# Second mixture of experts: three quarters of its routing moved into the attention stage before it, and its gathers cut into groups of eight

## The reference, cut to what matters

```python
# fifth: causal attention, 16 heads of 16, keys and values from the first 512 rows of ctx
q, k, v = layernorm(x) @ Wq.T + bq, ctx @ Wk.T + bk, ctx @ Wv.T + bv
x = x + softmax(mask(q @ k.T / 4)) @ v @ Wo.T + bo
# sixth: mixture of 8 experts, every row goes to its two best, and a shared expert for all rows
xf = layernorm(x).reshape(2048, 256)
shared = gelu(xf @ Wfc_s + bfc_s) @ Wproj_s + bproj_s            # hidden width 1024
topk_p, topk_i = top_k(softmax(xf @ Wr), 2); gate = topk_p / sum(topk_p)
routed = sum over e of gate[:, e] * (gelu(xf @ Wfc[e] + bfc[e]) @ Wproj[e] + bproj[e])
x = x + shared + routed
```

## Time and profile before

| | us |
|---|---|
| median of 3 runs | 3063.31 (3052.5 to 3068.39) |
| the profiled execution | 3049.62 |
| its span, first to last instruction | 3047.9 |
| attention stage's last addition to `x` ends | 2540.8 |
| first matmul on a shared item | 2564.8 |
| last (fifth) early shared item done | 2673.5 |
| first and last routed tile copied out | 2709.3, 2978.2 |
| last shared item done | 3033.1 |

### The profile page before, as it was taken

How to read it: one execution, slowest core, us unless ns; L and a number is a source line. 1 busy time by engine, 2 the same in 40 slices (tenths; PEclk the granted TensorE clock), 3 DMA queues, 4 the chain that set the end, 5 groups by cost and what they waited for, 6 DMA issues and landing times.

```text
span 3047.9 us, 31366 instructions
## 1 busy us (share of the span) xinstructions
PE 2437.6 (80%) x10876; PEld 1587.8 (52%) x10876; DVE 2186.9 (72%) x3129; ACT 1445.5 (47%) x2547; POOL 888.9 (29%) x614
## 2 busy tenths in 40 slices
PE   4988886478888899938982798897669797699996
PEld 1333432367766566727872234333224345689995
DVE  5999999598886564337885799999845443467775
ACT  5656563145554222214653665665214344256672
POOL 2778776000000000020002487777402121400004
PEclk8999999799999899968995899999968877789997
DMA  4033030700000000022421220312075400236652
GB/s 163 2 110 110 1 112 0 243 22 1 22 1 1 33 1 1 0 102 104 140 80 56 111 97 14 111 43 69 28 153 111 89 2 30 104 129 220 222 204 87
DMA packets 89233, 238.55 MB, mean 78 GB/s; under 512 B 9474, under 2 KB 52879, under 8 KB 81256
## 3 DMA queue, kind: packets, MB, share of 16 engines
q1 hardware_dynamic: 72708, 211.64, 21.6%
q0 software_dynamic: 4608, 12.59, 1.3%
q10 hardware_dynamic: 11760, 12.32, 1.3%
HBM read 194.42 MB, written 42.09 MB: 78 GB/s over the span
## 4 chain that ended last, share of the span: by engine, by line
PE 46%; DVE 28%; ACT 10%; issue 9%; DMA 3%; POOL 3%; ACTq 1%; SPq 1%; DVEq 0%; POOLq 0%
DVE psum L633 10%; PE psum L107 6%; PE psum L108 6%; PE psum L109 6%; PE psum L430 5%; PE psum L114 3%; DVE ch L641 3%; PE psum L395 2%; PE psum L1233 2%; PE psum L1247 2%; ACT g L3024 2%; PE psum L1217 2%; PE psum L1195 1%; PE psum L2358 1%; ACT WH L2874 1%
## 5 line engine op out<-in xcount | busy, mean ns | idle before, releaser
L315 POOL TENSOR_TENSOR bu<-u,row 128x1024 f32<-128x1024 f32 x254 | 597.8, 2358 | 288.0 <-DVE psum L633 189.1
L430 PE MATMUL psum<-ch,ident 128*128 128x512 f32 x1024 | 511.3, 628 | 138.8 <-DVE ch L641 138.2
L633 DVE TENSOR_TENSOR_SCAN psum<-psum,bu 128x1024 f32<-128x1024 f32 x256 | 585.4, 2287 | 19.0 <-ACT psum L512 18.8
L430 PEld LDWEIGHTS psum<-ch,ident 128*128 128x128 f32 x1024 | 188.6, 196 | 428.2 <-DVE ch L641 246.0
L512 ACT ACTIVATE psum<-dt,A 128x511 f32<-128x511 f32 x512 | 332.3, 682 | 0.4
L641 DVE TENSOR_TENSOR ch<-psum,row 128x1024 f32<-128x1024 f32 x256 | 313.0, 1223 | 7.6
L1503 POOL IOTA i<- 128x128 f32 x2 | 0.7, 346 | 766.6 <-DVEq L3172 766.6
L3024 ACT ACTIVATE g<-psum,bias 128x256 f32<-128x256 f32 x248 | 101.2, 471 | 210.3 <-PE psum L109 130.5
L395 PE MATMUL psum<-hT,inw 128*128 128x512 f32 x256 | 138.2, 672 | 43.2 <-ACT sz L472 27.3
L107 PE MATMUL psum<-WH,hs 128*128 128x256 f32 x496 | 145.2, 293 | 15.0 <-DVE hs L3109 6.0
L3109 DVE TENSOR_TENSOR hs<-g,hs 128x512 fp32r<-128x512 f32 x124 | 85.9, 693 | 91.1 <-ACT hs L3031 82.6
(11 more groups left out here) (376 smaller groups left out, 5885.8 us busy)
## 6 DMA issues: line engine op xcount, KB each, us to landing
W<-in_m1W SPq DMA_DIRECT2D x25, 2052.0 KB, 8.7
row<-Ascr SPq DMA_DIRECT2D x64, 512.0 KB, 4.8
row<-Bscr SPq DMA_DIRECT2D x64, 512.0 KB, 4.8
W<-in_m0W SPq DMA_DIRECT2D x16, 1024.0 KB, 9.3
k<-x1scr SPq DMA_DIRECT2D x16, 384.0 KB, 6.7
q<-x1scr SPq DMA_DIRECT2D x16, 384.0 KB, 9.2
x1scr<-hi SPq DMA_DIRECT2D x48, 128.0 KB, 2.4
m1buf<-zt SPq DMA_DIRECT2D x23, 256.0 KB, 3.5
```

The costliest lines, as they stand in the source:

```text
L315: e.tensor_tensor(m.bu[i % 3][:, :, :], u, m.row[:, g, 0, :, :], ALU.mult).then_inc(*m.fed.up)
L430: p = pe.matmul(m.y, k.ident, m.ch[i % RING_C][:, j, :], start=False, stop=g == UNITS - 1 and j == 1)
L633: dve.tensor_tensor_scan(flat, flat, m.bu[i % 3][:, :, :].rearrange("p a n -> p (a n)"), 0.0, ALU.mult, ALU.add).then_inc(*m.scan.up)
```

## The change

- The DRAM buffer `m1buf` has room for all 2048 rows for each expert (`ROOM`), and 256 more. The slot of a row is then `2048 * expert + rank`, and needs only the batches up to its own. Clearing it, early in the kernel, takes 16,640 rows instead of 5,888.
- For batches 0, 1 and 2 the layer norm, the logits, the two best, the ranks and the scatter stand inside the attention stage: units "r" (turn), "l" (logits), "n" (ranks) of batch b-1 in period b, and eight scatters on POOL in the slots of `X1_SENT`. The order of the other units in period 1 is new (`x1_period`): the maxima are woven in faster at the end, keys and queries come later. In period 3 the units spread over 22 slots instead of 14.
- The shared expert's weights are loaded and split in period 3 (`X1_SPLITS`). `WH` shares its space with one set of queries and keys.
- The mixture stage begins with the norm of the last batch only; its routing is for that batch, with eight scatters. `EARLY` is 3 instead of 5, so that five shared items stand behind the routed ones. The turn of the first routed tile moved behind the bias of the gates. SP reads the place of each tile's rows from `rsi`.
- All gathers have buffers of their own. They go out in four groups of eight; three of the groups wait for a place in the shared items. The additions on DVE are four tiles behind each of the last four shared items, instead of three behind each of the last three and seven at the end.

```diff
+ROOM = N
...
+    for j in range(E + 1):
+        n = min(ROOM, ROOM * E + 256 - ROOM * j) // 128
+        sp.dma_start(k.DR["m1buf"][ROOM * j:ROOM * j + 128 * n, :].rearrange("(t p) c -> p t c", p=128),
+                     k.zt[:, 0:1, :].to_broadcast([128, n, D])).then_inc(*k.cleared["m1"].up)
...
+def route_rows_dve(k, m, dve, b):
+    dve.wait_ge(*k.inv_dev(20 + b))
+    for t in range(4 * b, 4 * b + 4):
+        normed(dve, m.FN[:, t, :], k.X[:, t, :], k.xmv, k.xrs, t).then_inc(*m.fn_in.up)
+def logits_pe(k, m, pe, rT, bank):
+    for t in range(4):
+        for j in range(2):
+            p = pe.matmul(bank[:, E * t:E * t + E], rT[:, j, 128 * t:128 * t + 128], m.wr[:, j, :], start=j == 0, stop=j == 1)
+    return p
...
+def marks_dve(k, m, dve, b):
+    v = k.v
+    s = slice(4 * b, 4 * b + 4)
+    o1, o2 = m.oo[:, 0, s, :], m.oo[:, 1, s, :]
+    first_of_four_dve(k, m, dve, m.lg[:, s, :], m.m1[:, s], o1)
+    dve.scalar_tensor_tensor(out=m.l2[:, :, :], in0=o1, scalar=-3e38, in1=m.lg[:, s, :], op0=ALU.mult, op1=ALU.add).then_inc(*v.up)
...
+    first_of_four_dve(k, m, dve, m.l2[:, :, :], m.m2[:, :], o2)
+    dve.tensor_tensor(m.both[:, s, :], o1, o2, ALU.add).then_inc(*m.marks.up)
+    dve.tensor_tensor(m.lg[:, s, :], m.lg[:, s, :], wide4(m.m1[:, s]), ALU.subtract).then_inc(*m.below.up)
+def ranks1_pe(k, m, pe, b, bank):
+    pe.wait_ge(*m.marks(b))
+    rows = m.both[:, 4 * b:4 * b + 4, :].rearrange("p t e -> p (t e)")
+    pe.matmul(bank[:, 0:32], m.tri[:, :], rows, start=True, stop=True)
+    return pe.matmul(bank[:, 32:64], m.ones[:, :], rows, start=True, stop=True)
+def slots_dve(k, m, dve, b, bank, signal):
+    v = k.v
+    for t in range(4):
+        n = 4 * b + t
+        dve.tensor_tensor(m.tot[:, n + 1, :], m.tot[:, n, :], bank[:, 32 + E * t:32 + E * t + E], ALU.add).then_inc(*v.up)
+        dve.wait_ge(*v.last())
+    s = slice(4 * b, 4 * b + 4)
+    dve.tensor_tensor(m.rk[:, :, :], m.tot[:, s, :], bank[:, 0:32].rearrange("p (t e) -> p t e", e=E), ALU.add).then_inc(*signal.up)
+    dve.wait_ge(*signal.last())
+    dve.tensor_tensor(m.two[:, :, :, :], m.oo[:, :, s, :], m.rk[:, :, :].unsqueeze(1).to_broadcast([128, 2, 4, E]), ALU.mult).then_inc(*v.up)
+    dve.wait_ge(*v.last())
+    dve.tensor_reduce(m.sl[:, :, s], m.two[:, :, :, :], AX, ALU.add).then_inc(*v.up)
+    dve.wait_ge(*v.last())
+    dve.tensor_copy(m.si[:, :, s], m.sl[:, :, s]).then_inc(*m.put.up)
+def scatter_pool(k, m, pool, b, i):
+    t, j = 4 * b + i // 2, i % 2
+    if i == 0:
+        if b == 0:
+            pool.wait_ge(*k.cleared["m1"](E))
+        pool.wait_ge(*m.fn_in(4 * b + 3))
+        pool.wait_ge(*m.put(b))
+    pool.indirect_dma_start(k.DR["m1buf"], bass.IndirectOffsetOnAxis(ap=m.si[:, j, t:t + 1], axis=0), m.FN[:, t, :], None) \
+        .then_inc(*m.sent.up)
...
+PAUSE = ("-", 0, 0)
+def x1_routing(b):
+    return [("r", b, 0), ("r", b, 1)], [("l", b, 0)], [("n", b, 0)]
 def x1_period(b):
-    end = x1_end(b - 1) if b else x1_values(1)
-    ahead = x1_keys(b + 2) + x1_queries(b + 2) + x1_values(b + 2) if b + 2 < B else []
-    return x1_woven(x1_maxima(b + 1) if b + 1 < B else [], end + ahead)
+    maxima = x1_maxima(b + 1) if b + 1 < B else []
+    if b == 0:
+        return x1_woven(maxima, x1_values(1) + x1_keys(2) + x1_queries(2) + x1_values(2))
+    turned, logits, ranks = x1_routing(b - 1)
+    if b + 2 < B:
+        q, kk = x1_queries(b + 2), x1_keys(b + 2)
+        rest = turned + kk[0:1] + logits + kk[1:2] + q[0:2] + ranks + q[2:4] + x1_values(b + 2)
+        return x1_woven(maxima[0:24], x1_end(b - 1)) + x1_woven(maxima[24:], rest, 4)
+    return x1_woven(maxima, x1_end(b - 1) + 2 * [PAUSE] + turned + [PAUSE] + logits + 3 * [PAUSE] + ranks)
...
-X1_LAST = [28, 28, 28, 14]
+X1_LAST = [28, 28, 28, 22]
...
+X1_SPLITS = [20, 22, 24, 26]
+X1_SENT = {(b + 1, 28 + i): (b, i) for b in range(2) for i in range(4)}
+X1_SENT.update({(b + 2, i): (b, 4 + i) for b in range(2) for i in range(4)})
+X1_SENT.update({(B - 1, 24 + i): (B - 2, i) for i in range(8)})
...
+    elif w == "r":
+        for t in range(4):
+            pe.wait_ge(*k.route.fn_in(4 * b + t))
+            p = turn_in(k, pe, bank[:, 128 * t:128 * t + 128], k.route.FN[:, 4 * b + t, 128 * j:128 * j + 128])
+    elif w == "l":
+        for i in range(2):
+            pe.wait_ge(*x1_drawn(m, ("r", b, i)))
+        if b == 0:
+            pe.wait_ge(*k.route.w_r(0))
+        p = logits_pe(k, k.route, pe, m.oT, bank)
+    elif w == "n":
+        if b == 0:
+            pe.wait_ge(*k.route.consts(2))
...
+                quarter_act(k, k.route, act, 0, X1_SPLITS.index(s))
...
+            route_rows_dve(k, k.route, dve, b)
+    elif w == "r" and j == 1:
+        dve.wait_ge(*m.full(n))
+        dve.tensor_copy(m.oT[:, 1, :], bank).then_inc(*m.by_dve.up)
+    elif w == "l":
+        dve.wait_ge(*m.full(n))
+        logits_dve(k, k.route, dve, b, bank, m.by_dve)
+        dve.wait_ge(*x1_drawn(m, u))
+        if b == 0:
+            dve.wait_ge(*k.route.consts(2))
+        marks_dve(k, k.route, dve, b)
+    elif w == "n":
+        dve.wait_ge(*m.full(n))
+        slots_dve(k, k.route, dve, b, bank, m.by_dve)
...
+            if b == B - 1 and s in X1_SPLITS:
+                if s == X1_SPLITS[0]:
+                    dve.wait_ge(*m.sc(32 * (B - 1) - 1))
...
+                scatter_pool(k, k.route, pool, *X1_SENT[b, s])
...
-EARLY = 5
...
+EARLY = 3
...
+    for i in range(8):
+        scatter_pool(k, r, pool, B - 1, i)
...
+    pool.wait_ge(*r.sent(2 * NT - 1))
+    pool.wait_ge(*m.gi_in(0))
...
+        if x and x % 4 == 0:
+            pool.wait_ge(*(m.hd(4 * (LATE + 1) + 2), m.hd(4 * (LATE + 2) + 3), m.half(LATE + 3))[x // 4 - 1])
...
+            pool.indirect_dma_start(m.R[2 * x + j], None, k.DR["m1res"], bass.IndirectOffsetOnAxis(ap=m.gi[:, j, x:x + 1], axis=0)) \
+                .then_inc(*m.back[x].up)
...
-    weights(0)
...
+        n = sp.value_load(m.rsi[0:1, t:t + 1], min_val=0, max_val=E * ROOM // 256)
+        sp.dma_start(m.xe[t % 3][:, :, :], parts[bass.ds(n, 1), :, :, :].rearrange("n p a c -> (n p) a c")).then_inc(*m.xe_in[t % 3].up)
...
-    for q in range(3):
-        quarter_act(k, m, act, 0, q)
...
+    x_stats_act(k, act, 20 + B - 1)
...
-    dve.wait_ge(*m.vecs(0))
-    for b in range(B):
-        dve.wait_ge(*k.inv_dev(20 + b))
-        for t in range(4 * b, 4 * b + 4):
-            normed(dve, m.FN[:, t, :], k.X[:, t, :], k.xmv, k.xrs, t).then_inc(*m.fn_in.up)
-    for q in range(3):
-        quarter_dve(k, m, dve, 0, q)
+    x_stats_dve(k, dve, 20 + B - 1)
+    x_inverse_dve(k, dve, 20 + B - 1)
+    route_rows_dve(k, m.r, dve, B - 1)
...
-        if n >= LATE:
-            if n == LATE:
+            turned(n + 1)
+        if n > LATE:
+            if n == LATE + 1:
                 dve.wait_ge(*m.gates(0))
                 dve.wait_ge(*m.x_g(2 * B - 1))
-            for _ in range(3):
+            for _ in range(4):
```

418 lines of the change are left out of this document (231 added, 187 removed).

## The result

| | before | after |
|---|---|---|
| median (us) | 3060.52 of 4 runs (3052.5 to 3068.39) | 3013.1 of 4 runs (3000.56 to 3017.55) |
| profiled execution, its span | 3049.62, 3047.9 | 3017.55, 3015.7 |
| attention stage's last addition ends | 2540.8 | 2578.65 |
| first product, counted from there | 24.0 | 5.8 |
| first routed copy, counted from there | 168.5 | 89.9 |

The ratio of the times is 0.9849, 95% interval 0.9825 to 0.9873. The profiled executions differ by 32 us, the medians by 47: the one of before was its kernel's fastest, the one of after its slowest. Further down, one execution of late_adds (3138.89 us, at a mean clock of 0.79 against 0.90 in its others) was in a slower state and is left out of that kernel's median.

The account below looks back on a forecast made before the run. PE bounds the routed stretch, so gains lie around it: opening -76.2, tail -4.3, slowing +5, attention stage +30, sum -45.5 us. That gave span 3002, profiled execution 3004, and with 13.7 for the median 3017; range 2988 to 3042.

Parts of the forecast that it names:

- Opening and early items: From the attention stage's last addition to the first routed copy: T + 92.3 against 168.5 us, -76.2.
- Tail: From the last routed copy to the span's end: 65.4 us against 69.7, -4.3, before any slowing by gathers.
- The slowing by groups of eight: In the tail, PE slowed by indirect transfers: +5 us for five groups, bounds 0 and 37.
- The sign named for it: In the tail, a sign expected if right: tail 65 us with no stretch of 10 us under 60 matmuls.
- The rival that groups of eight slow PE as one row does: In the tail, four gather groups act as one row of 32, losing 20 to 30 us: 3040; chance 0.17.
- Attention stage: Routing work, scatters and weight casts moved into this stage lengthen it by 30 us, bounds +12 and +45.
- Period 3: In the attention stage: POOL's scatters between cuts +6.5, four scatters at its start +2, weight casts and new units +4.5 us.
- my fourth rival: The clock falls in the attention stage, costing PE up to 30 us more: 3047 and above; chance 0.07 with other losses.
- The step on the maxima's trip: End of period 1: the 20 us trip does not shrink; later query unit and four scatters sharing DMA engines add 5 us.
- The rule on the shared port: Attention stage: VectorE and GpSimd lock a shared port, so 24 moved scatters cost 13 us on POOL, the sum 4 higher.
- Every indirect transfer stalls PE: Rival for all 64 scatters and gathers: 73 us in place of 5, making it slower, 3085; chance 0.05.
- Clearing: Early clearing of the larger DRAM buffer, 11 MB more: fits a DMA gap at 0 us; without the gap 30.

Follow-up runs that it names:

- late_adds: The changed kernel with the additions of four tiles of gathered rows half an item later on DVE, behind the next item's splits; 2998.41 us.
- after_again: The changed kernel run again unchanged, on the chip type whose kernel before took 3030.09 us; 3008.35 us.
- scatters_back: The changed kernel with all 32 scatters in one row behind the barrier again, routing of three batches still early; 2989.67 us, on another chip 3025.8.
- max_early: The changed kernel with batch 2's maxima stored to DRAM earlier on SP's queue in period 1, their load back not moved; 3013.95 us.
- routing_late: scatters_back with period 1 in its old order, batch 0's routing in period 2 and that of batches 1 and 2 in period 3; 3017.97 us.
- no_groups: The changed kernel without the three waits between groups of eight gathers, on the same chip as after_again; 3005.73 us.
- after_again2: The changed kernel run a third time unchanged, on a chip whose kernel before took 3053.63 us; 3012.37 us.
- no_groups2: The same kernel as no_groups, without waits between the groups of gathers, on the same chip as after_again2; 3043.17 us.

## Why the prediction was right, and where its steps did not

Forecast 3017, measured 3013.1; the change of the medians is -47.4, and -46.3 was forecast (from the median of 3063.31 that was then known). The sum of the steps did less well than the median. It gave -45.5 between profiled executions, and those differ by -32.1: -78.6 in the opening (forecast -76.2), +35.0 in the attention stage (+30), +8.9 in the tail (+0.7), +2.8 ahead of the attention stage (0) and -0.3 in the routed tiles. I then added to the new kernel the 13.7 us by which the median of before lay above its profiled execution; after's lies 4.4 below its own, because its profiled execution was its slowest. By its steps:

- **Opening and early items**: right. First product 5.8 us behind the last addition (forecast 4.7), the first item done at 25.0 (25.4), the third at 52.3 (53.8), the first routed copy at 89.9 (92.3), -78.6 for -76.2. The second item took longer than forecast (17.7 for 15) and the third less (9.6 for 14.4); on B they took 15.5 and 11.9, the same sum. 18.2 of the 78.6 us lie ahead of the first product. How the other 60 divide between the two items fewer, the routing that moved and the shorter row of scatters was not tried singly.
- **Tail**: the full-pace part was right, 66.9 on chip B for 65.4. The slowing by groups of eight was taken as +5 and was 11.3 (78.2 less 66.9), inside its bounds of 0 to 37. The sign named for it, no stretch of 10 us under 60 matmuls, failed: there are 48 in 2966 to 2976. The reason given, that one group before had done no harm, looked only at whether PE's next item was on time. The second group starts 1.5 us behind the first, and the late item that it meets takes 16.5 us, but too short a pause is not the whole of it: the fourth group starts 10.8 us behind the third, and its item takes 15.6 us where it takes 12.1 on B. There the second quarter of the item's first products is done at 2994.34, and ACT, which waits for it with its gelu, starts 6.1 us later, 1.6 us behind the end of the group (the releaser in the brackets had long been done):

```profile
2988.92 0.95 POOL L3043 DMA_INDIRECT R<-m1res,gi  x1 [10.77 <-PE psum L111]
...
2994.06 0.28 PE L111 MATMUL psum<-xT,WH 128*128 128x256 f32 x1
...
3000.43 1.57 ACT L3221 ACTIVATE g<-psum,bias 128x256 f32<-128x256 f32 x4 [4.97 <-DMA row<-Ascr]
```

In after_again, on B, with the same group going out from 2987.62 on, the gelu starts 0.08 us behind the products:

```profile
2992.77 0.28 PE L111 MATMUL psum<-xT,WH 128*128 128x256 f32 x1
...
2993.13 0.83 ACT L3221 ACTIVATE g<-psum,bias 128x256 f32<-128x256 f32 x2
```

The rival that groups of eight slow PE as one row does is false all the same: the row of 32 costs 33 us (99.7 less 66.9), eight in a group cost a third of that, and four cost nothing.
- **Attention stage**: +35.0 for +30. Period 1 +11.0 for 9.8, with 11.2 us of waiting for the maxima for the 14 forecast and 2.5 for a cut of POOL's. Period 2 +4.4 for 7.5. Period 3 +21.2 for 13.0 is the term that was mis-sized. I had PE with room there and POOL as the limit. With the scatters it took 63.2 to 68.6 us in seven executions, with them back behind the barrier 55.0 and 55.8, so they account for 7 to 14 where 8.5 was forecast. The other 7.5, from the 47.5 of before to 55.0, are the norm, logits, ranks and the casts of weights, for which 4.5 was forecast. The clock, which was my fourth rival, is how much of this shows: PE is busy at 0.60 in after, at 0.81 in scatters_back and at 0.89 in before. Whether the scatters lowered it by the waits that they made, or otherwise, is not shown.
- **The step on the maxima's trip** came out in its number and not in its reason. I took 20 us as the way of one small transfer through queue and DRAM. max_early shows that whichever half of the trip leaves behind the loads of keys and queries takes 9 to 11 us and that the other takes 2 to 3, so that moving the store alone gains nothing. With the old order of period 1 and no routing in it (routing_late) the wait is 9.2 us; which of the two shortens it was not separated.
- **The rule on the shared port** (the Trainium skill, SBUF — State Buffer, section on the two separate sides): a longest scatter of 1.88 us in period 3 (POOL's timeline above) is the direction it gives, but the median of all is 0.98 against 0.96, and the 24 moved scatters together last 1.4 us more than 24 at that median. The price of 0.53 us for each, 13 us in all, did not come. By that section of the Trainium skill the lock concerns DVE's operations in a two-port mode or with two inputs from SBUF, which the prediction left out.
- **"Every indirect transfer stalls PE"** is false: on B none does, and on A PE itself keeps its pace through the first nine of a row. That they do no harm can't be said of A: in the fourth group above, the fifth gather is going out when the products are done that ACT learns of 6.1 us later.
- **Clearing** at nothing: the page of after has DMA shares of 6 and 5 tenths in the eighth and ninth fortieth and 0 behind them, where before has 7 and 0: it fits the gap. The attention stage began at 2281.8 against 2279.0, in other executions of the same program between 2265.8 (max_early) and 2282.4, so that a cost of a few us can't be told from that spread. It was not tried alone.

What the forecast owes to luck: on chip B the same change gave 3030.09 to 3008.35, 22 us, and on A, in the third set, 3053.63 to 3012.37, 41 us, not 47. On B there was nothing to win from cutting the rows, judging by no_groups and scatters_back (the kernel before has no profile on B). The median's hit rests further on the two profiled executions lying at opposite ends of their kernels' runs, as said above. And my profile of before held both prices, the loss in the rows and the gain in cover, without saying which of them goes with the chip.

A part of the profile's account stays uncertain. Period 1 of one program (after, after_again, after_again2, no_groups, no_groups2, late_adds) lasted 86.9 to 100.2 us. Period 1 of no_groups2, beside the second row of the first fence:

```profile
2354.49:2454.72 100.23, 81.19 (x410) 39.16 (x410) 44.20 (x113) 31.93 (x51) 19.33 (x37) 0.69 0.36 75
```

66.64 us busy at a clock of 0.85 and 81.19 at 0.69 are the same work, 56.6 and 56.0 us at full clock (estimates), and the rest of the period is 20.3 and 19.0. So the whole 13.3 us is the granted clock. Before had 0.91 there in both profiles; why the new order of period 1 is granted less, and so unevenly, is open.

## What to carry to other kernels

Ask of a moved step what it really waits for. Room for every row made the slots of three batches known early. Sending those rows early as well was not needed on B, because POOL stood idle behind the barrier; on A the row of 24 that replaced them cost 19 us in the opening and gave back 8 to 13 in period 3, and groups of four scatters cost 10. The gain itself is argued from the stages; no run took the early slots away. Judge an experiment by the stage that it changes: late_adds was 10 us faster, and the part that it changed had given one of them. And look at a long row of indirect transfers on more than one chip before it is called harmless or harmful; groups of four gathers with a wait on PE's progress between them cost nothing on chips where groups of eight cost 11 us. And where the profile says that an engine waits for nothing, look who makes what it reads next.
